# Two score products from twin weights, softmax denominators turned inside PSUM, and other orders for four engines

## The chip, the cores and the metric

The kernel runs on one NeuronCore of a Trainium2 chip. Five engines work at once, each through a list of its own: TensorE (PE, matrix products; PEld is its weight load), VectorE (DVE), ScalarE (ACT), GpSimd (POOL) and SyncE (SP, here only transfers). They wait for one another by semaphores. SBUF is the working memory; the eight banks of PSUM take what PE writes. The metric is the device time of one launch, in microseconds (us).

## The reference, cut to what matters

The input is 16 sequences of 256 tokens, 128 channels, all fp32. Four layers follow one another, each with a layer norm before it and another on its result, and a residual sum:

```python
x = x + norm(long_conv(norm(x)))     # e: recurrence over time, done with two scans
x = x + norm(moe_top2(norm(x)))      # l: router of 8 experts, gate/up/down, a shared expert
x = x + norm(attention(norm(x)))     # a: 16 heads of 64, causal, with 2 null keys and values per head
x = x + norm(four_experts(norm(x)))  # f: router of 4, top 2
# inside attention
q = l2norm(q) * q_scale;  k = l2norm(k) * k_scale
sim = 8 * q @ concat(null_k, k).T + alibi
out = softmax(sim) @ concat(null_v, v) @ w_out
```

## The kernel before

Sixteen sequences are taken two at a time: a group `g` is 512 tokens, four tiles of 128, and there are 8 groups. The four layers are steps named e_, l_, a_ and f_, and the kernel is a pipeline over groups: in one turn of the middle loop the engines work on layer a of group i, on f of group i-1, on l of group i+1 and on e of group i+2. Setting up the weights consists of steps s_.

What each engine does and in which order stands in lists written out in the program: PROLOGUE, FIRST (a of group 0), MIDDLE (run five times), LAST_L, LAST_A and LAST_F, each with a list for PE, DVE, ACT and POOL. `a_mix.3` is step `a_mix` with argument 3. An engine never leaves the order of its list, so a step that waits holds up all behind it.

**Split products.** A product that has to be exact is made of three fp32r products: `mm3` adds high x high, high x low and low x high. The router scores of layer l (`l_route`: 8 columns for each tile, into bank 3) and the scores against the null keys (`a_null`: 32 columns for each tile) are such products with a narrow right side, so each costs 12 products and 12 weight loads of 128x128 a group. DVE then copies them out of PSUM (L1478 to `logit0`, L1544 to `null_s`). `logit0` goes through `l_pick` (the two best, L1488 is its last instruction), an exponential on ACT (`l_exp`, L1105) and `l_coef`.

**Attention.** A group has 8 units `c` of four heads of one sequence. For each unit PE makes the scores (`a_scores`, L2003 and L2009), ACT the exponentials (L1188 to L1197), scaled by the key roots `rnorm[:, 0]`, POOL masks them (L941) and adds two blocks (L951), PE makes row sums with a matrix of ones into bank 7 (L2050, L2053) and the products with the values (L2060, L2062), and DVE's `a_mixes` does six things: it turns the row sums in blocks of 32x32 from bank 7 into SBUF (L1591, `den_rows`), adds the null part (L1596, `den`), inverts (L1600), spreads and turns the inverse (L1602), scales the product (L1605, `qT<-bank,mixed`), and scales the unit's null shares (L1608, 128x16). After the last unit of a sequence the shares are turned (L1611). PE's row sums of the next unit wait until L1591 has read bank 7. The null part is made ready once a group in `a_nT` (DVE L1582 turns it, L1585 adds pairs into `null_sum`).

**Roots.** Inverse roots are powers of -0.5 on POOL: of queries (L928), of keys (`k_norms`, L933, 128x32, twice a group, `a_kss.0` and `a_kss.1`), and of the norms' variances (L885, L892). `keep_x2` (`a_keep`) copies a tile on POOL. `f_bias` (L972, L976) weighs biases there.

**Others named below.** `l_norm` (L1383, `xn<-x`) waits for POOL's root of n_l. `s_flo` (L1362) splits three weights once, on DVE. `s_warm` issues five idle products of 512 columns on PE (L1772). `f_clock` does the same (L2094) at the start of each turn from group 1's.

Of the kernel before, what the change touches and what calls it, by code (L numbers as in the profile page):

```python
# [59 lines left out]
a_m.0 a_m.1 a_null a_k.0 a_k.1 a_t.0 a_m.2 a_kr.0 a_k.2 a_k.3 a_t.1 a_kr.1 a_kt a_m.3 l_turn2 a_v.0 a_t.2 a_v.1  # L60
a_t.3 l_turn3 a_v.2 a_v.3 l_route l_g.0 a_scores.0 l_u.0 l_g.1 a_nT l_u.1 l_cT a_scores.1 l_g.2 a_mix.0 l_u.2 l_c.0
a_scores.2 a_mix.1 l_c.1 e_turn1 a_scores.3 l_g.3 l_c.2 a_mix.2 a_scores.4 a_mix.3 l_u.3 l_g.4 a_scores.5 a_mix.4
l_u.4 l_c.3 a_scores.6 a_mix.5 l_down.0 a_scores.7 a_mix.6 l_down.1 l_down.2 l_down.3 a_mix.7 a_out.0 a_out.1 l_x.0
l_x.1
# [13 lines left out]
a_ss.0 a_ss.1 a_ss.2 l_turn2 a_ss.3 l_res a_kss.0 a_kss.1 e_stats a_scores.0 a_scores.1 a_scores.2 a_scores.3 e_scan
a_scores.4 a_scores.5 a_scores.6 a_scores.7 l_dstats.1 l_dstats.0 a_keep l_astats.0 l_astats.1 a_o.0 a_o.1
# [5 lines left out]
f_clock a_m.0 a_m.1 a_null a_k.0 f_turn.0 f_turn.1 f_ce.0 f_ce.1 a_k.1 f_sw.0 f_me.0 a_kr.0 a_t.0 a_m.2 a_k.2 f_ceT  # L85
f_sw.1 a_k.3 f_relu.0 f_relu.1 f_sw.2 a_kr.1 a_t.1 a_m.3 a_kt a_v.0 f_me.1 l_turn2 f_ce2 a_t.2 f_sw.3 a_v.1 a_t.3
a_v.2 f_ml.0 f_ml.1 f_ce2T f_ml.2 f_ml.3 a_v.3 f_out.0 l_turn3 a_scores.0 l_route f_out.1 f_out.2 a_nT l_g.0 f_out.3
a_scores.1 l_u.0 l_g.1 a_mix.0 a_scores.2 a_mix.1 l_u.1 e_turn1 l_cT a_scores.3 l_g.2 l_u.2 a_mix.2 a_scores.4
a_mix.3 l_g.3 l_u.3 l_c.0 a_scores.5 a_mix.4 l_g.4 l_c.1 a_scores.6 l_c.2 l_u.4 a_mix.5 l_c.3 a_scores.7 a_mix.6
l_down.0 l_down.1 l_down.2 l_down.3 a_mix.7 a_out.0 a_out.1 l_x.0 l_x.1  # L90
# [12 lines left out]
a_v.3 l_turn3 a_scores.0 l_exp l_g.0 a_scores.1 l_g.1 a_scores.2 l_cT a_scores.3 l_g.2 a_scores.4 l_g.3 a_scores.5
# [11 lines left out]
f_clock a_m.0 a_m.1 a_null a_k.0 a_k.1 f_turn.0 f_turn.1 f_ce.0 f_ce.1 f_sw.0 a_t.0 a_m.2 a_kr.0 f_sw.1 f_me.0 f_ceT  # L115
a_k.2 f_sw.2 f_relu.0 f_relu.1 a_k.3 f_ce2 a_kr.1 f_sw.3 a_t.1 a_kt a_m.3 a_v.0 l_turn2 f_ce2T a_t.2 f_ml.0 f_ml.1
f_me.1 f_ml.2 f_ml.3 a_v.1 f_out.0 f_out.1 a_t.3 l_turn3 a_v.2 a_v.3 l_route a_scores.0 l_g.0 f_out.2 f_out.3 a_nT
a_scores.1 a_mix.0 l_g.1 l_cT a_scores.2 a_mix.1 l_u.0 l_g.2 a_scores.3 l_c.0 a_mix.2 l_u.1 l_c.1 a_scores.4 a_mix.3
l_g.3 l_u.2 a_scores.5 l_g.4 l_u.3 a_mix.4 a_scores.6 l_c.2 a_mix.5 l_u.4 l_c.3 a_scores.7 a_mix.6 l_down.0 l_down.1
# [2105 lines left out]
```

## Time and profile before

| | |
|---|---|
| median of 3 runs | 960.9 us (960.82 to 961.22) |
| profiled execution, its own time | 960.52 us |
| its span, first to last instruction | 958.4 us |
| PE busy | 881.4 us, 92% |
| DVE busy | 787.3 us, 82% |
| ACT busy | 589.4 us, 61% |
| POOL busy | 556.2 us, 58% |
| mean granted TensorE clock | 0.991 of full |
| DMA over the span | mean 12 GB/s |

The span is 2.1 us shorter than the execution's own time; what lies outside is the launch and the end. Matrix products are pipelined, so a row's duration of a product is longer than the step from one to the next, and a busy PE isn't one at its peak: the steps have to be read from start times. A group takes about 110 us in the middle of the run.

### The profile page before, as it was taken

The page shows a single profiled execution, that of the slowest core. Times are in us where ns is not written, and L with a number is a line of the kernel's source. Part 1 is how long each engine was busy: PE and PEld are TensorE (multiplying, and loading weights), DVE is VectorE, ACT ScalarE, POOL GpSimd, SP SyncE. Part 2 cuts the span into 40 slices and gives each one's busy share as a digit, 9 for nine tenths or more (in the row PEclk, how much of TensorE's full clock was granted, in tenths as well). Part 3 has the DMA queues.
Part 4 walks back from the last instruction along what each step waited for, and adds up shares of the span by engine and source line. Part 5 has one row for each costly group of instructions (what it writes and reads, how often), then busy time and mean ns, then how long its engine had stood idle before and what let it go on. Part 6 is the DMA issues. An engine that isn't in the chain of part 4 may idle for free.

```text
span 958.4 us, 21520 instructions
## 1 busy us (share of the span) xinstructions
PE 881.4 (92%) x8149; PEld 704.7 (74%) x8149; DVE 787.3 (82%) x2505; ACT 589.4 (61%) x1255; POOL 556.2 (58%) x487
## 2 busy tenths in 40 slices
PE   0887899998999999999999989999999999999886
PEld 0575678687787878787686968778687877878666
DVE  7885898789988899879997899988998688965576
ACT  4529673975558662875729664685728775686731
POOL 4235854586646954567635856468635864467623
PEclk9989899999999999999999999999999999999999
DMA  6400000000000000000000000000000000000000
GB/s 160 109 1 0 12 2 2 1 13 1 13 2 1 12 2 13 1 12 2 2 12 1 13 2 13 1 1 12 2 13 1 1 2 13 1 1 1 13 2 11
DMA packets 21991, 11.46 MB, mean 12 GB/s; under 512 B 7552, under 2 KB 21248, under 8 KB 21760
## 3 DMA queue, kind: packets, MB, share of 16 engines
q1 hardware_dynamic: 20032, 9.50, 3.6%
q8 instruction: 64, 1.05, 0.5%
q10 hardware_dynamic: 1856, 0.59, 0.3%
q14 instruction: 39, 0.32, 0.1%
HBM read 7.99 MB, written 2.10 MB: 11 GB/s over the span
## 4 chain that ended last, share of the span: by engine, by line
PE 44%; DVE 43%; issue 5%; ACT 4%; POOL 3%; DMA 0%; DVEq 0%; ACTq 0%; POOLq 0%
PE bank L1752 7%; PE bank L1754 6%; PE bank L1753 6%; PE bank L1759 4%; DVE x4m L1704 3%; PE bank L2075 2%; PE bank L2003 2%; DVE mixed L1602 2%; DVE conv L1435 2%; DVE unit L1512 2%; DVE mixed L1591 2%; DVE qT L1605 2%; DVE den L1596 2%; DVE sumsq L1553 2%; DVE xn L1383 2%
## 5 line engine op out<-in xcount | busy, mean ns | idle before, releaser
L928 POOL TENSOR_TENSOR rnorm<-sumsq,minus_half 128x16 f32<-128x16 f32 x32 | 93.8, 2932 | 66.6 <-DVE sumsq L1556 66.5
L1191 ACT ACTIVATE square<-bank,bias_k,rnorm 128x256 f32<-128x256 f32 x128 | 65.7, 571 | 52.8 <-PE bank L2003 52.8
L2003 PE MATMUL bank<-qT,kT 64*128 64x256 f32 x512 | 97.4, 388 | 0.0
L2009 PE MATMUL bank<-qT,kT 64*128 64x128 f32 x512 | 84.0, 284 | 4.5 <-ACT unit L1197 2.8
L933 POOL TENSOR_TENSOR rnorm<-unit,minus_half 128x32 f32<-128x32 f32 x16 | 86.8, 5430 | 0.1
L2009 PEld LDWEIGHTS bank<-qT,kT 64*128 64x128 f32 x512 | 71.0, 186 | 17.3 <-issue 5.6
L941 POOL TENSOR_SCALAR_AFFINE_SELECT unit<-unit 128x512 f32<-128x512 f32 x64 | 40.5, 638 | 62.1 <-ACT unit L1197 62.1
L941 POOL TENSOR_SCALAR_AFFINE_SELECT square<-square 128x512 f32<-128x512 f32 x64 | 44.5, 695 | 55.1 <-ACT square L1197 55.1
L1121 ACT ACTIVATE xaT_hi<-bank 128x256 fp32r<-128x256 f32 x16 | 5.9, 384 | 110.8 <-PE bank L1920 110.6
L2003 PEld LDWEIGHTS bank<-qT,kT 64*128 64x128 f32 x512 | 68.8, 186 | 0.3
L1191 ACT ACTIVATE unit<-bank,bias_k,rnorm 128x256 f32<-128x256 f32 x96 | 51.4, 573 | 28.5 <-PE bank L2003 28.5
L2075 PE MATMUL bank<-w_out,qT 128*128 128x128 f32 x512 | 63.4, 277 | 1.7 <-DVE qT L1605 1.7
L2075 PEld LDWEIGHTS bank<-w_out,qT 128*128 128x128 f32 x512 | 59.7, 192 | 3.6 <-DVE qT L1605 2.0
L1197 ACT ACTIVATE unit<-bank,bias_k,rnorm 128x128 f32<-128x128 f32 x128 | 52.8, 478 | 0.0
L1197 ACT ACTIVATE square<-bank,bias_k,rnorm 128x128 f32<-128x128 f32 x128 | 52.5, 473 | 0.0
L1157 ACT ACTIVATE qT<-bank,qk_scale 128x512 f32<-128x512 f32 x64 | 40.5, 687 | 17.3 <-PE bank L1759 17.2
L1759 PEld LDWEIGHTS bank<-ident,unit 128*128 128x128 f32 x296 | 33.0, 142 | 20.1 <-issue 8.6
L1553 DVE TENSOR_REDUCE sumsq<-square 128x16 f32<-128x1024 f32 x32 | 38.9, 1215 | 9.6 <-ACT square L1137 9.6
L1605 DVE TENSOR_TENSOR qT<-bank,mixed 128x512 f32<-128x512 f32 x64 | 44.2, 691 | 2.2
L1130 ACT ACTIVATE unit<-bank 128x512 f32<-128x512 f32 x64 | 37.3, 599 | 13.9 <-PE bank L1754 12.5
L1570 DVE TENSOR_TENSOR unit<-unit,rnorm 128x1024 f32<-128x1024 f32 x32 | 39.0, 1222 | 7.4 <-POOL rnorm L928 7.4
L1759 PE MATMUL bank<-ident,unit 128*128 128x128 f32 x296 | 40.1, 276 | 5.1 <-ACT val L1164 2.3
(424 smaller groups left out, 2969.0 us busy)
## 6 DMA issues: line engine op xcount, KB each, us to landing
xin<-in_L_attn_x SPq DMA_DIRECT2D x7, 256.0 KB, 2.8
out<-x SPq DMA_DIRECT2D x7, 256.0 KB, 2.3
square<-in_L_attn_w_kv SPq DMA_DIRECT2D x1, 1024.0 KB, 6.2
unit<-in_L_attn_w_q SPq DMA_DIRECT2D x1, 512.0 KB, 5.8
w_out<-in_L_attn_w_out SPq DMA_DIRECT2D x8, 64.0 KB, 2.1
xin<-in_L_attn_x ACTq DMA_DIRECT2D x1, 256.0 KB, 3.1
unit<-in_L_ffn_experts_gate ACTq DMA_DIRECT2D x1, 256.0 KB, 3.4
unit<-in_L_ffn_experts_up SPq DMA_DIRECT2D x1, 256.0 KB, 2.9
```

What stands on the lines that cost most here:

```text
L928: pool.tensor_tensor(rnorm[:, 1, t, :], sumsq[:, t % 2, :], minus_half[:], ALU.pow).then_inc(a_root.sem, 1)
L933: pool.tensor_tensor(rnorm[:, 0, ts, :], k_sumsq[:, ts, :], minus_half[:].unsqueeze(1).to_broadcast([P, 2, H]), ALU.pow).then_inc(a_kroot. ...
L941: pool.affine_select(out=pd, in_=pd, compare_op=ALU.is_ge, fill=0.0, base=0, pattern=[[0, 4], [1, P]], channel_multiplier=-1).then_inc(a_m ...
L1191: last = act.activation(early(pr, j), k0, ACT.Exp, bias=bias_k0[:, h:h + 1], scale=by)
L1197: last = act.activation(late(pr, j), bank[2][:, 2 * P * s + P * j:2 * P * s + P * (j + 1)], ACT.Exp, bias=bias_k1[:, h:h + 1], scale=by)
L1553: V.tensor_reduce(sumsq[:, t % 2, :], square[:, 2 * (t % 2):2 * (t % 2) + 2, :].rearrange("p j (h d) -> p (j h) d", d=DH), AX_X, ALU.add). ...
L1605: V.tensor_tensor(outT[:, 2 * q:2 * q + 2, half(b)], pv_bank(g, c)[:].rearrange("p (f n) -> p f n", f=2), rec_cols.unsqueeze(1).to_broadca ...
L1752: mm(dst, left.hi, right.hi, start=True, stop=False)
L1759: last = nc.tensor.transpose(dst[:, t * P:(t + 1) * P], src(t), ident[:])
L2003: return mm(bank[s][:, 2 * P * i:2 * P * (i + 1)], kT[rs, p, 2 * P * b:2 * P * b + P], qT[rs, p, 2 * P * b:2 * P * (b + 1)], start=True, s ...
L2009: return mm(bank[2][:, 2 * P * s + P * i:2 * P * s + P * (i + 1)], kT[rs, p, ts], qT[rs, p, ts], start=True, stop=True)
L2075: mm(out_bank(g, h)[:, ts], outT[:, c, ts], w_out[:, c, :], start=(c == 0), stop=False)
```

## The change

1. `w0_router` and `w_nk` become `Twin` weights, with high and low part side by side. `mm_twin` makes one product of high x both parts and one of low x high that adds to the first half: 8 products and loads a group in place of 12, for the router and for the null keys each. The two halves are added by DVE while it empties the bank: a reduction over 2x32 values in place of the copy of 32, and over 2x128 in place of 128.
2. `den_rows` moves from SBUF to the second half of bank 7. L1591 turns from PSUM into PSUM, and `den` reads one operand from PSUM. PE's next row sums, and `e_turn1`, wait for `den` and no longer for L1591 alone.
3. The inverses of the four units of a sequence are kept (`recip` has four rows), and the null shares of all four are scaled by one instruction of 128x64 after the last, in place of four of 128x16.
4. `k_norms` works in four pieces of 128x16 in place of two of 128x32, and the exponentials wait for the piece that they need.
5. Two more `s_warm` steps stand in front of `l_x.0` and `l_x.1` of the prologue.
6. The lists of all stages are others. The steps are the same but for the pieces above.

```diff
+        class Twin(Split):
+            def __init__(self, name, width):
+                self.both = sb(name, [P, 2 * width], F32R)[:]
+                Split.__init__(self, self.both[:, 0:width], self.both[:, width:2 * width])
...
-        recip = sb("recip", [P, 2 * QW])
+        recip = sb("recip", [P, QW, 2 * QW])
...
-        den_rows, rec_cols = hid_sw[0][:, 0:2 * P], hid_sw[0][:, 2 * P:4 * P]
+        den_rows, rec_cols = bank[7][:, 2 * P:4 * P], hid_sw[0][:, 2 * P:4 * P]
...
-            def k_norms(g, b):
+            def k_norms(g, b, part):
                 pool.wait_ge(a_kss.sem, a_kss.at(g))
                 ts = slice(2 * b, 2 * b + 2)
-                pool.tensor_tensor(rnorm[:, 0, ts, :], k_sumsq[:, ts, :], minus_half[:].unsqueeze(1).to_broadcast([P, 2, H]),
+                hs = slice(H // 2 * part, H // 2 * (part + 1))
+                pool.tensor_tensor(rnorm[:, 0, ts, hs], k_sumsq[:, ts, hs], minus_half[:, hs].unsqueeze(1).to_broadcast([P, 2, H // 2]),
...
-                if c % (U // SEQ) == 0:
-                    act.wait_ge(a_kroot.sem, a_kroot.at(g, b + 1))
+                if c % 2 == 0:
+                    act.wait_ge(a_kroot.sem, a_kroot.at(g, c // 2 + 1))
...
-                V.tensor_copy(logit0[:], bank[3][:, 0:T * 8].rearrange("p (t e) -> p t e", e=8)).then_inc(s.sem, 1)
+                parts = bank[3][:, 0:T * 16].rearrange("p (t k e) -> p t e k", k=2, e=8)
+                V.tensor_reduce(logit0[:], parts, AX_X, ALU.add).then_inc(s.sem, 1)
...
-                V.tensor_copy(null_s[:], bank[3][:, 0:T * H * NULLS].rearrange("p (t h n) -> p t h n", h=H, n=NULLS)).then_inc(a_nullc.sem, 1)
+                parts = bank[3][:, 0:2 * T * H * NULLS].rearrange("p (t k c) -> p t c k", k=2, c=H * NULLS)
+                V.tensor_reduce(null_s[:].rearrange("p t h n -> p t (h n)"), parts, AX_X, ALU.add).then_inc(a_nullc.sem, 1)
...
-                if c:
-                    dve.wait_ge(a_nshare.sem, a_nshare.at(g, c))
+                if q == 0 and b:
+                    dve.wait_ge(a_nshare.sem, a_nshare.at(g, b))
...
-                share = null_rows.rearrange("p (k r) -> p k r", r=32)[:, blocks, NULLS * q:NULLS * q + NULLS]
-                V.tensor_tensor(share, share, recip[:].unsqueeze(2).to_broadcast([P, 2 * QW, NULLS]), ALU.mult).then_inc(a_nshare.sem, 1)
                 if q == U // SEQ - 1:
-                    dve.wait_ge(a_nshare.sem, a_nshare.at(g, c + 1))
+                    share = null_rows.rearrange("p (k r) -> p k r", r=32)[:, blocks, 0:QW * NULLS].rearrange("p k (q n) -> p k q n", n=NULLS)
+                    parts = recip[:].rearrange("p q k -> p k q").unsqueeze(3).to_broadcast([P, 2 * QW, QW, NULLS])
+                    V.tensor_tensor(share, share, parts, ALU.mult).then_inc(a_nshare.sem, 1)
...
+            def mm_twin(dst, left, twin):
+                width = twin.hi.shape[1]
+                mm(dst, left.hi, twin.both, start=True, stop=False)
+                return mm(dst[:, 0:width], left.lo, twin.hi, start=False, stop=True)
...
-                warm(bank[6], 5, w0_gate.hi)
+                warm(bank[0 if k > 3 else 6], 5, w0_gate.hi)
...
-                    pe.wait_ge(a_mix.sem, a_mix.at(g, 4 * c - 3))
+                    pe.wait_ge(a_tot.sem, a_tot.at(g, c))
```

Of the lists, the part of MIDDLE that lies around the middle of a turn (before, then after), in which most of what the text below speaks of stands:

```
DVE before: ... l_norm l_turn3 e_stats l_route l_pick f_out.0 f_out.1 e_apply f_out.2 l_hg.0 l_coef a_nT f_out.3 f_end_stats a_mix.0 ...
DVE after:  ... a_nexp l_norm l_turn3 e_stats l_route l_pick l_coef a_nT f_out.0 f_out.1 f_out.2 f_out.3 l_hg.0 f_end_stats e_apply a_mix.0 ...
ACT before: ... f_ml.3 a_nexp a_v.3 l_turn3 a_scores.0 l_exp l_g.0 ...
ACT after:  ... f_ml.3 a_v.3 a_nexp l_turn3 l_exp a_scores.0 l_g.0 ...
POOL before: ... a_ss.3 f_ce2 l_turn2 a_kss.0 l_res f_bias e_stats a_keep a_kss.1 a_scores.0 ...
POOL after:  ... f_ce_apply a_keep a_ss.1 a_ss.2 a_ss.3 a_kss.0.0 f_ce2 l_turn2 a_kss.0.1 l_res f_bias a_kss.1.0 a_kss.1.1 a_scores.0 e_stats ...
```

In PROLOGUE, DVE's `l_turn2` moves ahead of `s_w0`, and ACT's `s_null` ahead of `l_turn3`. In FIRST, DVE's `s_flo` moves from in front of `a_mix.0` to behind `a_mix.4`. In LAST_A, PE's `a_out.0` moves behind `a_mix.6`.

## Rows read from the trace of the kernel before

**Rows 1.** The page: busy us, share of the span, instructions, of all engines.

```profile
PE 881.4 (92%) x8149; PEld 704.7 (74%) x8149; DVE 787.3 (82%) x2505; ACT 589.4 (61%) x1255; POOL 556.2 (58%) x487
```

**Rows 2.** The page: shares of the chain that ended last, by engine.

```profile
PE 44%; DVE 43%; issue 5%; ACT 4%; POOL 3%; DMA 0%; DVEq 0%; ACTq 0%; POOLq 0%
```

**Rows 3.** Windows, middle turn: us, then busy PE, PEld, DVE, ACT, POOL, and clock.

```profile
383.80:431.00 47.20, 46.80 (x261) 35.70 (x262) 37.60 (x132) 39.72 (x75) 28.79 (x16) 1.00 0.02 7
431.00:495.10 64.10, 59.81 (x748) 50.26 (x745) 59.22 (x177) 31.23 (x77) 39.60 (x39) 1.00 0.02 6
```

**Rows 4.** Timeline of DVE in that turn: start us, us, line, operands.

```profile
442.17 0.16 DVE L1502 TENSOR_TENSOR prob<-exp,sum 128x8 f32<-128x8 f32 x1
...
443.86 1.34 DVE L1585 TENSOR_TENSOR null_sum<-mixed 128x64 f32<-128x64 f32 x1
...
467.92 1.02 DVE L1596 TENSOR_TENSOR den<-mixed,null_sum 128x8 f32<-128x8 f32 x1
...
470.37 1.17 DVE L1608 TENSOR_TENSOR mixed<-mixed,recip 128x16 f32<-128x16 f32 x1
```

**Rows 5.** Timeline of POOL in the same turn.

```profile
437.12 5.43 POOL L933 TENSOR_TENSOR rnorm<-unit,minus_half 128x32 f32<-128x32 f32 x1
...
443.82 1.29 POOL L951 TENSOR_TENSOR mixed<-unit 128x512 f32<-128x512 f32 x1
...
467.62 1.28 POOL L914 TENSOR_TENSOR conv<-conv,conv_b 128x512 f32<-128x512 f32 x1
...
470.21 1.29 POOL L951 TENSOR_TENSOR mixed<-square 128x512 f32<-128x512 f32 x1
```

**Rows 6.** Windows of L1596 alone, groups 0 to 6: us, busy us (count).

```profile
71.40:821.70 750.30, 18.49 (x56) 1.00 0.02 6
```

**Rows 7.** Windows of L1608 alone, groups 0 to 6.

```profile
71.40:821.70 750.30, 16.53 (x56) 1.00 0.02 6
```

**Rows 8.** Single lines of DVE: least, median and largest duration in ns.

```profile
L1596 DVE TENSOR_TENSOR den<-mixed,null_sum x64: 170/174/1017, 119.1 to 913.2; 128x8 f32<-128x8 f32 x64
...
L1608 DVE TENSOR_TENSOR mixed<-mixed,recip x64: 164/166/1192, 120.6 to 914.8; 128x16 f32<-128x16 f32 x64
...
L1605 DVE TENSOR_TENSOR qT<-bank,mixed x64: 690/691/692, 120.0 to 914.1; 128x512 f32<-128x512 f32 x64
...
L1585 DVE TENSOR_TENSOR null_sum<-mixed x8: 225/1335/1341, 110.3 to 878.9; 128x64 f32<-128x64 f32 x8
```

**Rows 9.** Timeline of PE: null scores, second and last of 12, then full products.

```profile
387.92 0.26 PE L1753 MATMUL bank<-w_nk_lo,xaT_hi 128*128 128x32 f32 x1
...
389.03 0.26 PE L1754 MATMUL bank<-w_nk_hi,xaT_lo 128*128 128x32 f32 x1
...
389.46 0.40 PE L1753 MATMUL bank<-xaT_lo,w_kv_hi 128*128 128x512 f32 x1
389.69 0.40 PE L1754 MATMUL bank<-xaT_hi,w_kv_lo 128*128 128x512 f32 x1
```

**Rows 10.** L1478, DVE's copy of the router scores: its waits (us, times).

```profile
  PE bank L1754: 1.7, 6
```

**Rows 11.** Timeline of PE behind the prologue: second and last product at the lower clock.

```profile
67.60 0.63 PE L1753 MATMUL bank<-w_q_lo,xaT_hi 128*128 128x512 f32 x1
...
70.95 0.40 PE L1752 MATMUL bank<-w_q_hi,xaT_hi 128*128 128x512 f32 x1
```

**Rows 12.** Timeline of PE, group 7: start of the second half of `a_out`.

```profile
914.89 0.38 PE L2075 MATMUL bank<-w_out,qT 128*128 128x128 f32 x1 [1.69 <-DVE qT L1605]
```

**Rows 13.** Groups by line and form: busy us, mean ns, idle before and releaser.

```profile
L1383 DVE TENSOR_SCALAR xn<-bank,n_y_mv,n_y_rstd 128x128 f32<-128x128 f32 x32 | 10.9, 400 | 2.3 <-POOL n_y_rstd L885 2.3
...
L1383 DVE TENSOR_SCALAR xn<-x,n_l_mv,n_l_rstd 128x128 f32<-128x128 f32 x32 | 8.9, 343 | 11.0 <-POOL n_l_rstd L885 10.8
```

**Rows 14.** Timeline of ACT in that turn: unit 0's first exponential and `l_exp`.

```profile
431.54 0.46 ACT L1188 ACTIVATE unit<-bank,bias_k,rnorm 128x128 f32<-128x128 f32 x1 [0.53 <-PE bank L2003]
...
435.70 0.23 ACT L1105 ACTIVATE exp<-exp 128x32 f32<-128x32 f32 x1 [0.35 <-DVE exp L1488]
```

More of the change, by code:

```diff
@@ L59 @@
     "PE": """
[L60 to L64, printed above, removed]
+a_m.0 a_m.1 a_k.0 a_null a_k.1 a_t.0 a_m.2 a_kr.0 a_k.2 a_k.3 a_t.1 a_kr.1 a_kt a_m.3 l_turn2 a_v.0 a_t.2 a_v.1
@@ L65 @@
+a_t.3 l_turn3 a_v.2 a_v.3 l_route l_g.0 a_scores.0 l_u.0 l_g.1 a_nT l_u.1 l_cT a_scores.1 l_g.2 a_mix.0 l_c.0
+a_scores.2 a_mix.1 l_g.3 e_turn1 l_c.1 a_scores.3 a_mix.2 l_u.2 a_scores.4 a_mix.3 l_g.4 l_u.3 l_c.2 a_scores.5
+l_c.3 l_u.4 a_mix.4 a_scores.6 l_down.0 a_mix.5 a_scores.7 l_down.1 a_mix.6 l_down.2 l_down.3 a_mix.7 a_out.0
+a_out.1 l_x.0 l_x.1
 """,
     "DVE": """
-a_ss.0 a_ss.1 a_null a_u.0 a_u.1 a_ss.2 a_kss a_u.2 l_turn2 a_ss.3 l_res a_u.3 l_norm l_turn3 a_nexp e_stats l_route
-l_pick l_coef l_hg.0 l_hu.0 a_nT e_apply l_hg.1 l_cT l_hu.1 s_flo a_mix.0 l_hc.0 l_hg.2 a_mix.1 l_hc.1 e_scan
@@ L84 @@
     "PE": """
[L85 to L89, printed above, removed]
@@ L90 @@
[L90 removed]
+f_clock a_m.0 a_m.1 a_k.0 f_turn.0 a_null f_turn.1 f_ce.0 f_ce.1 a_k.1 f_sw.0 f_me.0 a_kr.0 a_t.0 a_m.2 f_ceT a_k.2
+f_sw.1 f_relu.0 f_relu.1 a_k.3 f_sw.2 a_t.1 a_kr.1 a_m.3 a_kt f_sw.3 f_ce2 f_me.1 a_v.0 l_turn2 a_t.2 a_v.1 a_t.3
+a_v.2 f_ml.0 f_ml.1 f_ce2T f_ml.2 f_ml.3 a_v.3 f_out.0 l_turn3 a_scores.0 l_route f_out.1 a_nT f_out.2 f_out.3 l_g.0
+l_u.0 a_scores.1 l_g.1 l_cT a_mix.0 a_scores.2 a_mix.1 l_u.1 e_turn1 a_scores.3 a_mix.2 l_g.2 l_u.2 a_scores.4
@@ L91 @@
+a_mix.3 l_g.3 l_u.3 l_c.0 a_scores.5 l_g.4 a_mix.4 l_c.1 a_scores.6 l_c.2 a_mix.5 l_u.4 l_c.3 a_scores.7 a_mix.6
+l_down.0 l_down.1 l_down.2 a_mix.7 l_down.3 a_out.0 a_out.1 l_x.0 l_x.1
 """,
     "DVE": """
-f_stats.0 f_stats.1 a_null f_apply.0 f_apply.1 a_ss.0 f_turn.0 f_turn.1 f_route f_ce a_u.0 f_ce_apply a_ss.1 f_hid.0
-f_hid.1 a_u.1 a_ss.2 f_pick f_hid.2 a_u.2 a_kss a_ss.3 l_turn2 f_ce2 a_u.3 a_nexp f_hid.3 f_ce2_apply l_res l_norm
-l_turn3 e_stats l_route l_pick f_out.0 f_out.1 e_apply f_out.2 l_hg.0 l_coef a_nT f_out.3 f_end_stats a_mix.0 l_hu.0
@@ L114 @@
     "PE": """
[L115 to L119, printed above, removed]
@@ L120 @@
-l_down.2 l_down.3 a_mix.7 a_out.0 a_out.1 l_x.0 l_x.1
+f_clock a_m.0 a_m.1 a_k.0 a_null f_turn.0 f_turn.1 a_k.1 f_ce.0 f_ce.1 f_sw.0 a_t.0 a_m.2 a_kr.0 f_sw.1 a_k.2 f_me.0
+f_ceT f_sw.2 f_relu.0 f_relu.1 a_k.3 f_ce2 f_sw.3 a_kr.1 a_t.1 a_kt a_m.3 l_turn2 f_ce2T a_v.0 f_ml.0 f_ml.1 f_me.1
+f_ml.2 f_ml.3 a_t.2 a_v.1 f_out.0 f_out.1 l_turn3 a_t.3 a_v.2 a_v.3 l_route a_scores.0 f_out.2 a_nT l_g.0 f_out.3
+a_scores.1 l_u.0 l_g.1 a_mix.0 a_scores.2 a_mix.1 l_cT l_g.2 a_scores.3 l_u.1 a_mix.2 l_c.0 a_scores.4 l_g.3 l_u.2
@@ L121 @@
+a_mix.3 l_c.1 a_scores.5 a_mix.4 l_g.4 l_c.2 a_scores.6 l_u.3 a_mix.5 l_u.4 l_c.3 a_scores.7 a_mix.6 l_down.0
+l_down.1 l_down.2 l_down.3 a_mix.7 a_out.0 a_out.1 l_x.0 l_x.1
 """,
     "DVE": """
-f_stats.0 f_stats.1 a_ss.0 a_null f_apply.1 f_apply.0 a_ss.1 f_turn.0 f_turn.1 a_u.0 f_ce f_hid.0 f_ce_apply f_route
-f_hid.1 a_ss.2 f_hid.2 a_u.1 a_u.2 f_ce2 f_pick a_kss f_hid.3 f_ce2_apply a_ss.3 l_turn2 l_res a_u.3 l_norm a_nexp
-l_turn3 f_out.0 l_route l_pick l_coef f_out.1 f_out.2 l_hg.0 f_out.3 a_nT a_mix.0 l_hg.1 a_mix.1 l_cT l_hu.0
```

127 lines of the change are left out of this document (69 added, 58 removed).

## The prediction

> **What bounds the kernel now.** I read the page first. PE is busy 92% of the span and DVE 82% [rows 1], and the chain that ended last lies 44% on PE and 43% on DVE [rows 2]: two engines take turns as the bound. So I cut one middle turn in two by windows [rows 3]. From 383.8 to 431.0 PE is busy 46.8 of 47.2 us and DVE 37.6: PE bounds, DVE has 10 us to spare. From 431.0 to 495.1 DVE is busy 59.2 of 64.1 us. PE shows 59.8 there, but its rows are longer than its steps: a 512-column row lasts 0.40 and starts 0.23 behind the one before, a 32-column row lasts 0.26 and steps 0.111 ((389.03 - 387.92) / 10) [rows 9]. In this stretch PE has room, and ACT (31) and POOL (40) too. The chain of waits, followed through the same stretch, stays on DVE nearly all the way. What DVE saves there comes off the turn; what PE saves in the first stretch does too.
>
> Then I put DVE and POOL side by side. `den` normally takes 174 ns, at 467.92 it took 1.02 us and ended when POOL's L914 did (467.62 + 1.28 = 468.90). The null share at 470.37 took 1.17 us and ended with POOL's L951 (470.21 + 1.29 = 471.50), and `null_sum` at 443.86 took 1.34 and ended with the L951 of 443.82 [rows 4, 5]. All three have two operands in SBUF. L1605, with one in PSUM and one in SBUF, took 690 to 692 ns in all of its 64 runs [rows 8]. So a DVE instruction with two SBUF operands that starts under such a POOL instruction waits for its end, and one with a PSUM operand doesn't. POOL's powers don't hold DVE: L1502 took 0.16 us in the middle of a 5.43 us L933 [rows 4, 5].
>
> The Trainium skill ("SBUF — State Buffer", SBUF: two separate sides) says that VectorE and GpSimd share a port pair as an exclusive lock, taken by VectorE for an operation with two SBUF inputs against a GpSimd one that reads SBUF. The three waits agree; the free L1502 under a power, which reads SBUF too, doesn't.
>
> **The change part by part**, against the profiled execution's 960.5 us (0.4 under the median).
>
> *Denominator.* In groups 0 to 6, where DVE bounds, L1596 was busy 18.49 us in 56 [rows 6]; without waits it is 56 x 0.174 = 9.74. With its operand in PSUM it should never wait: **-8.7**. (Group 7's second stretch is left out: there ACT sets the pace.) At the other end it keeps waiting: 0.
>
> *Turning into PSUM.* No row shows DVE writing to PSUM. The nearest is what a PSUM source costs: 400 ns against 343 [rows 13], 57 ns. For the write of L1591 and the read of L1596 that is 2 x 56 x 0.057 = +6.4; the other end is 0, and no reason speaks for a gain. `den` has two operands like L1605, not one like L1383, and L1605's PSUM operand costs it nothing that varies [rows 8]: I take **0** and keep 6.4 for the range.
>
> The Trainium skill ("VectorE: DVE Perf Modes", The TRN2 errata) gives VectorE 120 cycles of fixed cost from PSUM and 58 from SBUF. That would be an estimated 65 ns for each `den`, 3.6 us in 56, and makes the sum that much smaller; rows 13 agree for instructions with one tensor operand (57 ns); for a write to PSUM no run here shows it yet.
>
> *Null shares.* L1608 was busy 16.53 us in 56 [rows 7], of which 56 x 0.166 = 9.3 without waits, so 7.2 of waiting. Of the 0.166 about 0.09 is a step, since the next instruction starts under it (56 x 0.09 = 5.0). Fourteen remain, of 64 values: 225 ns as L1585 without a wait [rows 8], a step of 0.15, 2.1 us; and at the present rate of waiting (7.2 / 56 = 0.13) 1.8 more. -7.2 - 5.0 + 2.1 + 1.8 = **-8.3**. If all fourteen wait like L1585 (1.11 each), 15.5 takes the place of the 1.8.
>
> *Null scores.* Four products a group less, 4 x 0.111 = 0.44 [rows 9], in the PE-bound stretch; the 64-column ones are still bound by the step of a weight load, I take it. 8 x 0.44 = **-3.5**. DVE's reduction of 256 values is some 0.13 longer and hides in DVE's 10 us of room; without it, +1.0.
>
> *Router scores.* Also 0.44, but DVE waited only 1.7 us in all for them [rows 10]; the reduction takes 0.03 x 8 back. **-1.4**.
>
> *`null_sum` moved.* L1585 waited 1.11 us in each of five middle turns. The new DVE list puts `a_nT` straight behind `l_coef`, and POOL's list has the second pair of key roots behind `f_bias`, about where the 5.43 us power ran from 437.12 [rows 5], which held nobody. I count half of 5.6, as POOL's hours shift too: **-2.8**, with 0 and -5.6 as ends.
>
> *Key roots in four.* Two pieces take at least the 5.43 us of the one that they replace, and a fixed part more, on POOL, which is busy 39.6 of 64.1 [rows 3, 5]. `a_kss.0.0` now stands before `f_ce2` and `l_turn2`, and only half of the roots stands before `l_res`, for whose root DVE waited 10.8 us in 7 times [rows 13]. That wait is covered: what needs `xn` is `l_turn3` on PE, which stands behind `f_out.0`, and PE was busy up to there. **0**; if PE comes earlier too, up to -10.8, and as much the other way if a root gets behind a piece.
>
> *PE's later permission.* The next row sums wait for `den` instead of L1591, 0.3 us later. Queued behind on PE are scores and layer l's products; PE has the room. **0**, 0.3 x 49 = 15 if PE had none.
>
> *Prologue.* Eight steps of 0.42 (67.60 to 70.95) at the lower clock [rows 11], against 0.23 at full [rows 9], so 1.2 GHz after PE had waited for `ce_rows` in front of `l_x.1`, 1.5 to 1.6 us in all. Ten more idle products fill that gap: **-1.6**, 0 if the clock falls all the same. `l_turn2` ahead of `s_w0` only swaps which of the two DVE waits with: 0. `s_null` ahead of `l_turn3` on ACT costs 0.6 at most, before a DVE wait: 0. `s_flo`'s 3.3 us stay in DVE's stretch: 0.
>
> *`a_out.0` behind `a_mix.6`.* DVE then finishes unit 6 earlier; `a_out.1` waited 1.69 us for DVE [rows 12]: **-0.6**, ends 0 and -1.7.
>
> *ACT.* `l_exp` now stands before `a_scores.0`. Before, unit 0's exponentials ran from 431.54 and `l_exp` at 435.70 [rows 14]. They took 3.8 (to 435.70 - 0.35). Now they start behind `l_exp`, at 435.93, and end at 439.7. `l_g.0`, POOL's mask of unit 0 and PE's `a_scores.1` wait for them; POOL's mask came only behind the power that ended at 442.55 [rows 5]: **0**, with 2.8 us of cover. `a_keep` moves ahead of three query roots, in POOL's waits of the first stretch (busy 28.8 of 47.2): 0, and one copy's time a turn if a root is late.
>
> Sum: 8.7 + 8.3 + 3.5 + 1.4 + 2.8 + 1.6 + 0.6 = 26.9. 960.5 - 26.9 = 933.6, at the median **934 us**.
>
> **The rivals.**
>
> *A, the waits move.* The lock isn't gone. If the fourteen shares all wait (+13.7 against my sum) and `null_sum` still waits (+2.8), the gain is 10.4: 950.5. For it: a share of 64 values is as exposed as L1585, which waited in five of eight. Against: L1608 was free in most runs.
>
> *B, the chain to the router shortens too.* POOL's earlier root takes DVE's 10.8 us: 923. For it: 1.5 us of waiting in each of seven groups. Against: PE reaches `l_turn3` no earlier but for the 0.44 of the null scores.
>
> *C, PE was the bound in both stretches.* Then only products count: 3.5 + 1.4 + 1.6 + 0.6 = 7.1, 954. For it: 59.8 of 64.1 busy; against: the steps.
>
> *D, slower.* ACT sits in `l_exp` with unit 0 behind it. Up to 2.8 us later than I reckon nothing happens; beyond that each us costs one in each of seven turns. From 2.8 + 26.9 / 7 = 6.6 us on it decides; at 8 us it would be 934 + 5.2 x 7 = 970. Against: `l_pick` stands directly behind `l_route` on DVE.
>
> *E, no change.* Turning into PSUM costs 26.9 / 56 = 0.48 us more each time; no row shows anything like it.
>
> **How the numbers follow.** Forecast (928 to 941) 0.46, A (941 to 951) 0.22, B (916 to 928) 0.14, C (951 to 958.9) 0.06, E 0.04, D 0.08. From 921 to 951 lie 0.46 + 0.21 + 0.13 = 0.80; it holds the price of PSUM (+6.4) and all shares waiting, and below most of B. A measurement of this kernel tells 0.2% (1.9 us) from no change. Faster 0.88, same 0.04, slower 0.08.
>
> **What the profile after would show.** L1596 with a largest duration near its median, L1591 no more than 60 ns longer; the shares 16 in number, few over 1 us; the stretch from `xlT_lo` to the next `f_clock` about 3.5 us shorter, the one before 0.4; eight products stepping 0.111 where there were twelve; L1585 at 0.23 in the middle turns. Wrong would make it: L1591 much over 0.5, DVE idle before `a_mix.0` or in `l_coef`, POOL late with a mask or a root, or PE idle before its row sums for `den`.

## The result, and the profile after

The changed kernel takes 936.16 us (median of 4 runs, 935.24 to 936.22), the kernel before 961.06 (4 runs) beside it: ratio 0.9739, 95% interval 0.9722 to 0.9756. The forecast was 934.0 with a range of 921 to 951. The sum came out 2 us too low; its terms, as the experiments show, were wrong by much more, in both directions, so that the closeness of the total is luck.

The page after, busy shares and then the shares of the chain that ended last; they answer to [rows 1, 2]:

```profile
PE 878.2 (94%) x8095; PEld 697.0 (75%) x8095; DVE 754.7 (81%) x2457; ACT 589.0 (63%) x1255; POOL 559.8 (60%) x503
...
PE 68%; DVE 19%; ACT 5%; POOL 4%; issue 3%; DMA 0%; DVEq 0%; ACTq 0%; POOLq 0%
```

DVE lost 33 us of work and more than half of its share of the chain. The same middle turn in windows (columns as in [rows 3]), then single lines of DVE (as in [rows 8]) and PE's null scores (as in [rows 9]):

```profile
371.60:418.40 46.80, 46.47 (x257) 35.23 (x258) 36.67 (x128) 39.76 (x75) 29.54 (x18) 1.00 0.02 7
418.40:477.90 59.50, 59.09 (x743) 49.30 (x740) 54.41 (x174) 30.94 (x77) 38.74 (x39) 1.00 0.02 6
```

```profile
L1606 DVE TENSOR_TENSOR den<-bank,null_sum x64: 166/167/168, 116.0 to 888.9; 128x8 f32<-128x8 f32 x64
...
L1601 DVE STREAM_TRANSPOSE bank<-bank x64: 433/459/466, 115.5 to 888.4; 128x256 f32<-128x256 f32 x64
...
L1620 DVE TENSOR_TENSOR mixed<-mixed,recip x16: 215/216/460, 131.5 to 890.4; 128x64 f32<-128x64 f32 x16
...
L1595 DVE TENSOR_TENSOR null_sum<-mixed x8: 226/226/227, 115.0 to 854.2; 128x64 f32<-128x64 f32 x8
```

```profile
377.56 0.28 PE L1770 MATMUL bank<-w_nk,xaT_hi 128*128 128x64 f32 x1
...
378.35 0.26 PE L1771 MATMUL bank<-w_nk,xaT_lo 128*128 128x32 f32 x1
```

The first stretch went from 47.2 to 46.8, the second from 64.1 to 59.5: 4.6 where about 3.5 was forecast. `den` never waits (largest 168 ns), nor does `null_sum`; of the sixteen shares the longest took 460 ns, 0.24 us more than the median. The eight products step (378.35 - 377.56) / 7 = 0.113.

The span is 23.9 us shorter. By the starts of `f_clock`, 3.06 us came off up to the first (162.09 to 159.03) and 22.7 in the six turns that follow (659.58 to 636.84), while the part behind the last became 1.9 longer (136.7 to 138.6, start of LAST_A's turn to the end). The 3.06 is no firm gain: f3_ending below runs the same program as the kernel after up to LAST_A, and its first `f_clock` came at 160.78, 1.75 later.

What I hadn't looked at before predicting is PE's own waits in one turn. Before, from 272.95 to 383.86, and after, from 265.40 to 371.63 (us in total, times, longest):

```profile
PE bank L2050 <- DVE x4m L1704: 1.7, 1, 1.7
PE bank L2050 <- DVE qT L1605: 1.4, 3, 0.6
PE bank L1905 <- DVE unit L1522: 1.1, 1, 1.1
PE bank L1752 <- DVE mixed L1694: 0.2, 1, 0.2
PE bank L2101 <- ACT conv L1203: 0.2, 1, 0.2
```

```profile
PE bank L2067 <- DVE conv L1438: 0.2, 1, 0.2
PE bank L1763 <- DVE mixed L1705: 0.2, 1, 0.2
```

By the timeline these are 4.63 us before and 0.45 after, in a turn that became 4.68 us shorter (110.91 to 106.23). The waits are a budget: as long as PE's own work stays as it is, no order and no DVE saving can take more out of a turn than PE waits in it. The turn less the waits fell only from 106.28 to 105.78. The eight products that went are worth 0.86 of that (106.64 in g2_no_twins, which has them back), and the new lists cost PE some 0.4 to 0.5 that is no listed wait (106.79 in f1_lists, which has the old operations); why isn't known.

### The profile page after: what moved, and what is told of

It is laid out like the page before. It is cut to its first block, busy times and chain, and to the rows that moved or that the text cites. A ratio compares the mean times of both kernels' runs of the same rounds, so it can differ in the third digit from the quotient of the medians.

```text
span 934.5 us, 21349 instructions
## 1 busy us (share of the span) xinstructions
PE 878.2 (94%) x8095; PEld 697.0 (75%) x8095; DVE 754.7 (81%) x2457; ACT 589.0 (63%) x1255; POOL 559.8 (60%) x503
## 3 DMA queue, kind: packets, MB, share of 16 engines
q8 instruction: 64, 1.05, 0.5%
## 4 chain that ended last, share of the span: by engine, by line
PE 68%; DVE 19%; ACT 5%; POOL 4%; issue 3%; DMA 0%; DVEq 0%; ACTq 0%; POOLq 0%
PE bank L1763 8%; PE bank L1764 6%; PE bank L1765 6%; PE bank L1776 5%; PE bank L2020 5%; PE bank L2077 4%; PE bank L1929 4%; PE bank L2194 3%; PE bank L2092 3%; PE bank L2200 3%; PE bank L2026 3%; PE bank L2079 2%; PE bank L2067 2%; PE bank L2196 2%; PE bank L2176 2%
## 5 line engine op out<-in xcount | busy, mean ns | idle before, releaser
L941 POOL TENSOR_TENSOR rnorm<-unit,minus_half 128x16 f32<-128x16 f32 x32 | 93.1, 2921 | 2.2 <-DVE unit L1572 2.2
L949 POOL TENSOR_SCALAR_AFFINE_SELECT square<-square 128x512 f32<-128x512 f32 x64 | 46.5, 730 | 48.0 <-ACT square L1205 48.0
L1580 DVE TENSOR_TENSOR unit<-unit,rnorm 128x1024 f32<-128x1024 f32 x32 | 40.9, 1280 | 10.0 <-POOL rnorm L935 10.0
L1172 ACT ACTIVATE val<-bank 128x512 f32<-128x512 f32 x64 | 37.3, 604 | 17.5 <-PE bank L1765 15.3
```

Of the source, the lines that this page charges most:

```text
L941: pool.tensor_tensor(rnorm[:, 0, ts, hs], k_sumsq[:, ts, hs], minus_half[:, hs].unsqueeze(1).to_broadcast([P, 2, H // 2]), ALU.pow).then_i ...
L949: pool.affine_select(out=pd, in_=pd, compare_op=ALU.is_ge, fill=0.0, base=0, pattern=[[0, 4], [1, P]], channel_multiplier=-1).then_inc(a_m ...
```

## The experiments

Times are medians; the ratio is to runs of the kernel before beside them, which took 960.53 beside the runs named e, 961.91 beside those named f and 960.71 beside those named g. The turn is the median of the five middle turns, from `f_clock` to `f_clock`; PE's waits are the sum over the second of these (272.95 to 383.86 in the kernel before).

| kernel | us | ratio (95%) | turn | PE waits |
|---|---|---|---|---|
| before | 961.06 | 1 | 110.86 | 4.63 |
| e1_den | 953.35 | 0.9924 (0.9911 to 0.9938) | 109.12 | 2.71 |
| e2_den_shares | 950.10 | 0.9892 (0.9877 to 0.9907) | 108.70 | 2.54 |
| e3_twins | 963.44 | 1.0034 (1.0023 to 1.0045) | 110.63 | 5.23 |
| e4_ops | 954.52 | 0.9938 (0.9925 to 0.9952) | 109.67 | 3.14 |
| g1_ops_fout3 | 956.97 | 0.9958 (0.9944 to 0.9972) | 109.85 | 4.24 |
| f1_lists | 957.01 | 0.9937 (0.9923 to 0.9951) | 110.15 | 3.25 |
| f2_den_back | 940.24 | 0.9774 (0.9760 to 0.9787) | 106.87 | 1.05 |
| g2_no_twins | 938.62 | 0.9778 (0.9763 to 0.9792) | 107.15 | 0.46 |
| g3_shares_unit | 947.76 | 0.9867 (0.9852 to 0.9882) | 108.32 | 2.46 |
| f4_nowarm | 937.74 | 0.9746 (0.9733 to 0.9759) | 106.29 | 0.46 |
| g4_out_swap | 938.37 | 0.9774 (0.9759 to 0.9790) | 106.28 | 0.44 |
| f3_ending | 934.61 | 0.9713 (0.9700 to 0.9726) | 106.31 | 0.46 |
| after | 936.16 | 0.9739 (0.9722 to 0.9756) | 106.32 | 0.45 |

### From the kernel before: the new operations in the old lists

**e1_den** is part 2 of the change alone.

```diff
-        den_rows, rec_cols = hid_sw[0][:, 0:2 * P], hid_sw[0][:, 2 * P:4 * P]
+        den_rows, rec_cols = bank[7][:, 2 * P:4 * P], hid_sw[0][:, 2 * P:4 * P]
...
-                        pe.wait_ge(a_mix.sem, a_mix.at(g - 2, 4 * ahead - 3))
+                        pe.wait_ge(a_tot.sem, a_tot.at(g - 2, ahead))
...
-                    pe.wait_ge(a_mix.sem, a_mix.at(g, 4 * c - 3))
+                    pe.wait_ge(a_tot.sem, a_tot.at(g, c))
```

> The kernel before with part 2 alone (row sums turned inside bank 7, PE's next row sums wait for den), old lists. Theory of the prediction: 8.7 us less, 952.2; the trace after shows the turn 17 ns longer in each of 56 units, which takes 1.0 back: 951.9 to 953.2. L1596's largest duration near its median of 0.17. Rival, the waits move: den no longer waits, but the reciprocal, the spread or the share behind it meets the same POOL instruction, or another engine is the bound anyway: 957 to 961. Rival, PE's later permission costs: slower than 961.

7.2 us less: the theory's mechanism, near its size. But it all came from the five middle turns (1.74 by the median, 7.4 over the five); LAST_L's turn, whose eight units the sum counted too, stayed at 105.98 (105.97 before). PE's waits in a turn fell from 4.63 to 2.71, and of 2.49 us between unit 0's and unit 7's `den` only 0.48 was left.

**e2_den_shares** adds part 3, the one share of 128x64 for four units.

> The kernel before with parts 2 and 3 (also the null shares once for four units), old lists. Theory: 8.7 + 8.3 = 17.0 less, 943.9, and 945 with the longer turn. Against the kernel with part 2 alone 8.3 less. Rival A (all shares wait 1.1 us each): 13.7 of that lost, 957 to 959. Rival, ACT or PE becomes the bound of the second stretch after some 10 us: 950.

Only 3.2 us more, not 8.3. Rival A is not the reason: the sixteen shares took

```profile
L1610 DVE TENSOR_TENSOR mixed<-mixed,recip x16: 212/215/1277, 134.3 to 903.6; 128x64 f32<-128x64 f32 x16
```

and 4.5 us in all. DVE got its time, but PE had hardly any waiting left to give back there: DVE's waits for PE between the two `den` rose from 0.9 to 1.7 us. The time is the second rival's (950), with PE as the engine.

**e3_twins** is part 1 alone, and **e4_ops** parts 1 to 3 together.

> The kernel before with the twin weights alone (both score products), old lists. Theory: null scores 3.5 and router scores 1.4 less: 956.0. If only the stretch in which PE bounds counts: 957.4. Rival C of the prediction (every product counts, also in the second stretch) gives the same here, so this run sizes the term. Rival, the reduction of 256 values sits in DVE's path and the product's gain is lost: 960 or more.

> The kernel before with parts 1 to 3 (all new operations, no pieces of the key roots, no idle products), old lists. Theory, the terms add: 8.7 + 8.3 + 3.5 + 1.4 = 21.9 less, 939.0, and 940 with the longer turn; the lists then are worth 3 to 4 us of the 24.8. Rival: the operations give only about half (948 to 950), because with the old lists PE or ACT takes over as the bound, and the lists give the other half.

Both theories missed on the twins: alone they made the kernel 2.9 us slower, on top of e2 4.4 slower, and e4_ops lies above its rival's 948 to 950 too. The rival of e3_twins, a reduction that costs DVE more than PE gains, names the right range (960 or more), but its reason doesn't hold: a turn by the median became 0.23 us shorter. PE does do less work, but in front of unit 0's row sums it waits until DVE has emptied `f_out.3` (L1704 before, L1712 here), which in the old DVE list stands behind `l_hg.0`, `l_coef` and `a_nT`. PE came earlier, so it waited longer there, 2.17 us in place of 1.74. The row names POOL's mask, which was ready in the same 0.1 us as DVE's L1712 (225.63 both); in the next turn it names L1712. The rows are from the first middle turn of e4_ops: the row sums, and then windows of 1 us (us, PE, PEld, DVE, ACT, POOL, granted clock):

```profile
225.78 0.43 PE L2064 MATMUL bank<-unit,ones 128*32 128x128 f32 x8 [2.17 <-POOL square L946]
```

```profile
225.00:226.00 1.00, 0.22 (x9) 0.25 (x13) 0.93 (x4) 0.42 (x1) 0.92 (x2) 1.00 0.00 0
226.00:227.00 1.00, 1.00 (x27) 0.72 (x22) 0.93 (x8) 0.00 (x0) 0.99 (x1) 0.68 0.00 0
227.00:228.00 1.00, 1.00 (x20) 0.84 (x16) 0.86 (x4) 0.00 (x0) 0.00 (x0) 0.50 0.00 0
228.00:229.00 1.00, 1.00 (x17) 0.46 (x9) 0.47 (x2) 0.00 (x0) 0.00 (x0) 0.50 0.00 0
229.00:230.00 1.00, 1.00 (x8) 1.00 (x10) 0.96 (x2) 0.00 (x0) 0.00 (x0) 0.62 0.00 0
```

Behind the wait the granted clock was at its lower level (0.50, 1.2 GHz) for some 3 us. That came in three of the five turns of e4_ops; these took 109.67 to 109.88 and the two others 108.44 and 108.46, so a fall costs 1.2 to 1.4 us here, 4.0 in all. Against e2's 108.70 the turns without a fall gained 0.25, where 0.6 was forecast. In e3_twins it came behind the same wait (2.18) in two of the five turns, which are 1.0 to 1.1 longer than the same turns of the kernel before, while the three others are 0.3 shorter. That makes 1.2 us of its 2.7 in the span; another 1.3 lie ahead of the first `f_clock`, as 1.7 of the 4.5 between e4_ops and e2 do. From one execution of each these can't be told from the variation of that part (1.75 us with the same instructions up to there, above).

**g1_ops_fout3** tries to take this wait out of e4_ops by one edit in DVE's list of MIDDLE:

```diff
- ... f_out.2 l_hg.0 l_coef a_nT f_out.3 ...
+ ... f_out.2 f_out.3 l_hg.0 l_coef a_nT ...
```

> The kernel of e4_ops with one edit in DVE's list of the middle turns: f_out.3 stands ahead of l_hg.0, l_coef and a_nT. In the trace of e4_ops PE waits 2.17 us in each middle turn in front of unit 0's row sums, until DVE has emptied f_out.3 (x4m ends at 225.64, the row sums start at 225.78), and in three of the five turns the granted clock is at its lower level for 3.4 us behind it, those turns being 1.4 us longer. Theory: the wait goes, so the three falls (4.2) go with it, and PE stands up to 2.2 us ahead for the rest of the turn, in which DVE has some 2.0 us to give: 1 to 2 us a turn in five turns; 954.5 - 4.2 - 5 to 10 = 940 to 945. Rival 1: DVE is the bound up to unit 0's den in any case, only the clock comes back: 950. Rival 2: the wait moves to POOL's mask, which was there at the same time: 953 to 955.

957.0: my theory fell, and all three guesses are under it. The wait for `f_out.3` is gone, but `l_coef` and `a_nT` come later and now meet POOL. DVE, then PE, in the second middle turn:

```profile
333.19 1.76 DVE L1506 TENSOR_TENSOR pick<-expert_no,idf 128x32 f32<-128x32 f32 x2
...
335.82 0.70 DVE L1589 STREAM_TRANSPOSE mixed<-bank 128x512 f32<-128x512 f32 x1
336.56 0.73 DVE L1592 TENSOR_TENSOR null_sum<-mixed 128x64 f32<-128x64 f32 x1
```

```profile
336.58 0.64 PE L2074 MATMUL bank<-unit,val 128*32 128x256 f32 x8 [1.78 <-DVE mixed L1589]
```

The pair of `pick` takes 0.26 in the kernel before (at 441.99, inside the power of [rows 5]) and 1.76 here, to 334.95; POOL was adding two blocks from 333.04 to 334.32 and masking to 334.91. PE now waits 1.78 for the null part's turn, then 1.33 for `qT`. The wait moved from one instruction to another; unit 0's `den` came 1.4 us later, and the turns took 109.83 to 110.09, as long as those of e4_ops with a fall, though the clock fell in only two of the five (behind that wait of 1.78). One edit in one list doesn't give what the new lists give.

### From the kernel after: one part undone in the new lists

**f1_lists** undoes parts 1 to 3: old operations, new lists.

> The kernel after with parts 1 to 3 undone: the old operations in the new lists, with the key roots in pieces and the added idle products. Theory: only null_sum's move (2.8, or 5.6 as the trace after has it at 0.23 in all turns) and the prologue (1.6) are left, and the ending loses 2: 955 to 958. Rival, the lists carry much of the gain by themselves: 950 or less. Rival, the new lists fit only the new operations: above 961.

Inside the range by the median, 4.9 under the 961.91 beside it (6.1 by the ratio). The lists (with parts 4 and 5) alone are worth 4.9, the operations alone 6.0, both 24.9. The remaining 14 us are in neither: each needs the other. Part 4, the key roots in pieces, was not tried by itself.

**f2_den_back** undoes the diff of e1_den in the kernel after.

> The kernel after with part 2 undone (the turned row sums in SBUF again, PE's next row sums wait for the turn alone). Theory: den waits for POOL again, about 8 us in 56: 943 to 945. If PE's later permission cost something in the new kernel, less: 938 to 942. Rival, in the second stretch PE and ACT now bound and DVE has room: 936 to 938.

4 us more by the medians, 0.35% by the ratios (3.4 us), and 3.6 by the sum of the turns, where the forecast had 8.7. The time lies in the range that I gave for a costly later permission of PE, but the trace has another reason: `den` waits again, but its 64 take 16.5 us, of which 16.5 - 64 x 0.174 = 5.4 is waiting; in the kernel before it was 10.4 (21.5 us). The old figure belonged to the old order, and PE's waits rose only from 0.45 to 1.05.

**g3_shares_unit** undoes part 3 in the kernel after.

```diff
...
+                share = null_rows.rearrange("p (k r) -> p k r", r=32)[:, blocks, NULLS * q:NULLS * q + NULLS]
+                V.tensor_tensor(share, share, recip[:, q, :].unsqueeze(2).to_broadcast([P, 2 * QW, NULLS]), ALU.mult).then_inc(a_nshare.sem, 1)
```

> The kernel after with the null shares scaled once for each unit again. Forecast's term: 8.3 more, 944.5. Theory now: PE is the bound also in the second stretch and DVE has 1.3 us of idle time between unit 0's and unit 7's den, which takes most of the 1.7 us that the shares cost DVE in a turn (8 x 0.09 of steps and 8 x 0.13 of waits for POOL, less the two large ones): 0.4 to 1 us in each of seven turns, 939 to 943. Rival, all of it fits in DVE's room: 936 to 937.

All three were wrong: 11.6 us more by the medians, 12.3 by the ratios, the largest term of all. In the new lists the shares of single units meet POOL far more often than in the old ones (median 166, 17.9 us in all):

```profile
L1618 DVE TENSOR_TENSOR mixed<-mixed,recip x64: 166/412/1232, 117.6 to 902.0; 128x16 f32<-128x16 f32 x64
```

Their sum is 29.1 us, against 3.9 for the sixteen in the kernel after. It is the lists that do this and not the other new operations: in f1_lists, with the old operations in the new lists, the 64 shares take 29.9. A second cost stood in no row of mine: the reciprocal waits on a semaphore for the share before, and DVE's idle time in front of L1610 is 6.4 us here and 2.7 in the kernel after. Together that is 28.9 us of DVE's path, more than its room. PE's waits in a turn rise from 0.45 to

```profile
PE bank L2066 <- DVE conv L1438: 0.9, 1, 0.9
PE bank L1921 <- DVE unit L1531: 0.7, 1, 0.7
PE bank L1762 <- DVE unit L1521: 0.4, 1, 0.4
PE bank L2066 <- DVE qT L1615: 0.3, 1, 0.3
PE bank L1762 <- DVE mixed L1704: 0.2, 1, 0.2
```

2.46, and the turn by 2.0.

**g2_no_twins** undoes part 1 in the kernel after.

> The kernel after with both twins undone (three products a piece again), new lists. In the trace after PE waits only 0.45 us in a middle turn, so every product should count: 8 x 0.111 in 7 or 8 turns, 6.2 to 7.1 more: 942.4 to 943.3. The forecast's terms (null scores 3.5, router scores 1.4): 941.1. Rival, as in the old lists, where the twins alone made the kernel 2.9 slower: 933 to 936.

938.62 lies between the theory's 942.4 and the rival's 936, and none of the three guesses holds. A middle turn is 0.85 us longer in the mean of five, about 8 x 0.111 = 0.89, with no more waiting of PE (0.46 against 0.45): in the new lists the products of both stretches count nearly in full. The medians differ by 2.5 and the ratios by 3.7; this kernel's first `f_clock` came at 156.85, 2.2 before that of the kernel after, and that covers half of the turns' 4.6. Nothing in the edit explains it. The granted clock was low in three places ahead of the first `f_clock` in the kernel after (63 to 67, 77 to 81, 100 to 105) and in two here (63 to 68, 94 to 98), and two executions of the same instructions differ there by 1.75 us (above), so I count it as variation, which isn't shown.

**f4_nowarm** takes `s_warm.4` and `.5` out of the prologue's list.

> The kernel after without the two added steps of idle products in the prologue. Theory: eight products step 0.42 in place of 0.23 again, 1.6 us more: 937.8. Rival, the clock falls or not whatever they do, or the time is covered by a wait behind it: 936.2.

Not told apart: 937.74 (936.26 to 938.08), ratio 0.9746 against 0.9739, spans equal at 934.5, first `f_clock` 0.3 later. The idle products do what they should, the first product behind them lasts 0.48 and not 0.79 us. Windows of 2 us of the kernel after show why little comes of it:

```profile
64.00:66.00 2.00, 2.00 (x7) 1.51 (x7) 1.93 (x7) 0.00 (x0) 1.00 (x1) 0.50 0.00 0
...
68.00:70.00 2.00, 2.00 (x11) 1.60 (x10) 1.71 (x7) 1.50 (x4) 0.00 (x0) 1.00 0.00 0
...
74.00:76.00 2.00, 0.99 (x4) 0.48 (x3) 0.96 (x3) 2.00 (x5) 2.00 (x2) 1.00 0.00 0
76.00:78.00 2.00, 1.27 (x7) 1.27 (x8) 1.01 (x2) 1.24 (x3) 2.00 (x1) 0.76 0.00 0
78.00:80.00 2.00, 2.00 (x8) 1.61 (x7) 0.00 (x0) 1.24 (x3) 0.28 (x1) 0.50 0.00 0
```

The eight products of the forecast do run at full clock, but behind the next stretch in which PE is half idle (74 to 78) the clock falls again, which it didn't at that place without them. One execution of each is little to go by: f3_ending, with the same idle products, had four such falls ahead of the first `f_clock` where the kernel after had three.

**g4_out_swap** puts `a_out.0` in front of `a_mix.6` again (LAST_A, PE), and **f3_ending** takes all lists of LAST_A and LAST_F as before.

> The kernel after with PE's a_out.0 in front of a_mix.6 in LAST_A again, nothing else. The forecast had 0.6 in favour of the new place: from the last f_clock to the end 139.2 in place of 138.6. Rival, the new place is what made the ending longer: 137 to 138. Second rival, POOL's f_end_stats behind a_scores.6 (2.97 us of DVE waiting in front of a_mix.6) did it, and the swap changes nothing: 138.6.

> The kernel after with the lists of the last turn and the last stage (LAST_A, LAST_F) as before (key roots in pieces). The ending behind the last f_clock took 138.7 us in the trace after and 136.8 in the trace of before, with 2.97 us of DVE waiting for POOL's root of f_end_stats in front of a_mix.6 and 1.2 for a_out.1. Theory: 1.9 less, 934.3. Rival, the ending is longer because of operations and not of order: 936 or more. The forecast itself had 0.6 in favour of the new order: 936.8.

From the last turn's `f_clock` to the end: 138.6 in the kernel after, 140.6 in g4_out_swap, 137.5 in f3_ending, 136.7 before. With `a_out.0` at its old place PE waits 2.09 us for unit 7's `qT` in front of `a_out.1`, and 1.21 in the kernel after. Behind it the clock falls, here; in the kernel after it is 1.00 in the same two windows:

```profile
892.00:894.00 2.00, 2.00 (x13) 2.00 (x12) 1.34 (x7) 0.00 (x0) 0.37 (x1) 0.57 0.00 0
894.00:896.00 2.00, 2.00 (x12) 2.00 (x12) 0.60 (x2) 0.00 (x0) 0.32 (x1) 0.58 0.00 0
```

So the new place is right and its own part is 0.9, near the 0.6 of the forecast; the other 1.0 is put down to that fall, from one trace of each. But the ending as a whole is longer than before, so the other new lists of it cost more than this gives. Where that begins shows on DVE, in front of unit 6:

```profile
882.50 1.43 DVE L1391 TENSOR_SCALAR x4m<-x4m,n_f_mv,n_f_rstd 128x128 f32<-128x128 f32 x4 [2.97 <-POOL n_f_rstd L892]
```

`f_end` stands before `a_mix.6` on DVE and needs POOL's root, which the new list of POOL has only behind `a_scores.6`; that this root is the whole of it was not tried. f3_ending beats both kernels by its median (934.61), but its interval and that of the kernel after overlap.

## Why the prediction was right, and what in it was not

**The bound.** "In this stretch PE has room" is the step that failed. PE's waits between unit 0's and unit 7's `den` were only 2.49 us in a turn; I had read room from the steps of a few products and not looked for the waits themselves. DVE's savings count until these are used up (e1: 1.7), and no longer (e2: 0.4 of the shares' 1.2). I summed DVE's terms as if they had no ceiling.

**Denominator**, -8.7: 7.2 in the old lists, 3.4 to 4.1 in the new. The mechanism holds: all 64 are 166 to 168 ns. The Trainium skill ("SBUF — State Buffer", SBUF: two separate sides) would have it so, and the trace agrees for this instruction; that powers on POOL hold nobody stays against it. The prediction had one row for that, an L1502 that ran in the last 0.4 us of a power [rows 4, 5], but the whole trace of the kernel before bears it out. I counted DVE's `tensor_tensor` instructions that began under a POOL instruction with more than 0.1 us of it left, and called one held if it took over 0.05 us more than the shortest of its line. With two SBUF operands all 23 under the two-input adds L914 and L951 were held, 24 of 31 under the masks L941, and none of 33 under the powers L928 and L933. With an operand in PSUM, under the same adds and masks, none of 65 was.

**Turning into PSUM**, 0 taken, 6.4 as the end: L1601 takes 459 ns against 442, `den` 167 against 174. 56 x (0.017 - 0.007) = 0.6. The Trainium skill ("VectorE: DVE Perf Modes", The TRN2 errata) gave an estimated 65 ns more for each `den`; the measurement, 7 less, decides against it for an instruction with one operand from PSUM and one from SBUF.

**Null shares**, -8.3: 3.2 in the old lists, 11.6 to 12.3 in the new. Mis-sized twice: the waiting was read off the old order (0.13 a share; in the new one 0.29), and the reciprocal's semaphore wait (0.06 a unit) was overlooked.

**Score products**, -3.5 and -1.4: in the new lists 4.6 over six turns (3.7 by the ratios), about the sum of both, since PE bounds the second stretch too, as rival C said. In the old lists +2.9, with the clock's falls in it: a rival that I didn't have.

**`null_sum`**, -2.8: it waits in no turn, so the upper end of 5.6 as far as DVE goes. Its worth by itself wasn't tried; the lists, with the key roots in pieces and the idle products, are worth 4.9 alone and 18.4 on top of e4_ops (954.52 - 936.16).

**PE's later permission and the key roots**, 0 and 0: PE waits 0.45 in a turn, for neither. **ACT**, 0: in the turn looked at, ACT stands 3.9 us waiting for DVE's `exp` in front of `l_exp`, and PE never waits for ACT in it: rival D's wait is there and its cover holds. **Prologue**, -1.6: 0.3 by the first `f_clock`, unresolved by the medians. **`a_out.0`**, -0.6: -0.9 by PE's wait, 1.9 with the clock, and +1.9 for the ending as a whole, which no term had.

**The rivals.** A: of the sixteen shares one waited, by 0.24 us. B: DVE's wait for POOL's root of n_l did fall, from 10.8 us to 3.9, but the stretch to `xlT_lo` is only 0.4 shorter, as forecast, so the wait was covered and B gives nothing. C: right on who bounds, wrong on the price, because it counted none of PE's 4.63 us of waits. E: 0.017 against the 0.48 that it needed.

So the total came out by luck, because errors cancelled: the terms' 21.9 for the operations were 6.0 in the old lists, and what the new lists do to PE's waits, 18.4 on top, was in the sum with 5.0. The better account is short: PE waited 4.63 us in a middle turn and now 0.45, which is 4.2 of the turn's 4.7; the rest is the products that went, less what the new lists cost PE.

## What to carry to other kernels

Before summing what a busy engine saves, list the waits of the other busy engine over one whole turn: their sum is the most that all savings on the first engine can give, and each names the list position to look at. Then treat the order of the lists and the cost of the operations as one change: here either alone gave 5 to 6 us, both 25, and an operation that does less (the twins) made the kernel slower in the old order, in part because the engine that it relieves then waited longer and its clock fell behind the wait. A wait for a shared resource belongs to an order, not to an instruction; read it again whenever the order changes.

## What the runs showed of the hardware

- DVE turns 128x256 from PSUM into the same bank of PSUM in 459 ns, against 442 into SBUF.
- The same 64 shares of 128x16 on DVE took 17.9 us in the old order of the lists and 29.1 and 29.9 in the new one (g3_shares_unit, f1_lists). With both operands in SBUF such an instruction was held by POOL up to 1.1 us (1.23 in place of 0.17); with one in PSUM `den` was held in none of 64 runs.
- POOL's two-input adds of 128x512 and its masks hold DVE's instructions with two SBUF operands (23 of 23 and 24 of 31 in the kernel before); its powers of 128x16 and 128x32, 2.9 and 5.4 us long, held none of 33.
- In e4_ops a wait of PE of 2.17 us was followed by some 3 us at the lower clock in three turns of five, costing 1.2 to 1.4 us each, and in two by none; in e3_twins it was two of five, and in g1_ops_fout3, behind waits of 1.76 to 1.78, two of five. In the kernel before, e1_den and e2_den_shares the wait in front of the row sums was 1.72 to 1.76 us and the clock stayed full in all five.
